# Two relational edge passes of a graph network: another order of ScalarE's work in a step

## The reference

```python
h = relu(layernorm(x))
for w, sl, b in ((w1, sl1, b1), (w2, sl2, b2)):      # two relational layers
    xt  = einsum('nd,rde->rne', h, w)                # 8 matrices, one for each type
    msg = xt[edge_type, src]
    h   = relu(segment_sum(msg, dst) + h @ sl + b)
x = x + h
h = relu(layernorm(x))
# a message layer follows: an MLP over (h[src], h[dst], edge_attr), a layer norm of the
# messages, a segment_sum, an MLP over the nodes and a last layer norm
x = x + message_layer(h, src, dst, edge_attr)
```

## Time and profile before

| | |
|---|---|
| runs, median | 2863.91 us |
| profiled execution | 2855.17 us, span 2853.5 us |
| busy in the span | PE 77%, DVE 71%, POOL 64%, ACT 54% |
| E1, 230 to 795 us | PE 494.08, DVE 425.04, ACT 326.71, POOL 383.09 us busy, granted clock 0.97, DMA share 0.49 |
| E2, 965 to 1520 us | PE 468.39, DVE 367.56, ACT 242.44, POOL 417.32 us busy, granted clock 0.96, DMA share 0.44 |

### The profile page before, as it was taken

The page is one execution under the profiler, slowest core; times in us unless marked ns, Lnnn a source line. Parts: engine busy times, 40 slices in busy tenths (PEclk is TensorE's granted clock), DMA queues, the critical chain, the costliest instruction groups (busy, mean ns, idle before and its releaser), DMA issues. The chain is left out here.

```text
span 2853.5 us, 54165 instructions
## 1 busy us (share of the span) xinstructions
PE 2187.5 (77%) x16219; PEld 1892.5 (66%) x16219; DVE 2023.0 (71%) x6854; ACT 1541.0 (54%) x3284; POOL 1821.7 (64%) x1381
## 2 busy tenths in 40 slices
PE   4778999999668899889873665577767766757997
PEld 4668988888668798888872565444444444435765
DVE  6887887878423587676755888676767676755999
ACT  5996656565423354444434877544334333425887
POOL 5763878765667188888866777288777777770000
PEclk9999999999889999999996888888888888888999
DMA  7994555545379644444437999666666666647998
GB/s 237 316 310 130 113 111 102 107 89 102 48 264 362 248 86 88 88 82 88 88 46 242 417 417 414 253 195 194 175 176 190 181 182 179 191 113 294 406 404 344
DMA packets 297971, 576.18 MB, mean 202 GB/s; under 512 B 65872, under 2 KB 147344, under 8 KB 297872
## 3 DMA queue, kind: packets, MB, share of 16 engines
q1 hardware_dynamic: 188112, 485.01, 46.9%
q0 software_dynamic: 109760, 90.00, 19.5%
HBM read 368.35 MB, written 206.50 MB: 201 GB/s over the span
## 5 line engine op out<-in xcount | busy, mean ns | idle before, releaser
L1056 POOL DMA_INDIRECT s<-E_summed,c_scat x392 | 652.1, 1664 | 262.6 <-ACT E_summed L1235 150.0
L1284 PE MATMUL ps<-c_w,E_masked 128*128 128x128 f32 x6272 | 722.6, 276 | 2.2 <-DVE E_masked L1087 2.0
L1284 PEld LDWEIGHTS ps<-c_w,E_masked 128*128 128x128 f32 x6272 | 714.1, 193 | 3.0 <-DVE E_masked L1087 3.0
L1087 DVE SCALAR_TENSOR_TENSOR E_masked<-E_type_row,E_hT 128x512 f32<-128x512 int32 x784 | 484.1, 688 | 74.4 <-ACT E_hT L1204 62.5
L365 POOL DMA_INDIRECT E_src_rows<-s,c_src x392 | 419.8, 1071 | 167.8 <-issue 118.0
L1418 POOL DMA_INDIRECT s<-E_summed,c_scat x196 | 335.8, 1713 | 126.3 <-issue 53.3
L1407 POOL DMA_INDIRECT E_ends<-h,c_near x196 | 220.1, 1123 | 91.0 <-issue 58.8
L1641 PE MATMUL ps<-E_same,E_normal 128*128 128x512 f32 (+3 forms) x392 | 175.1, 610 | 115.6 <-DVE E_normal L1501 115.6
L365 POOL DMA_INDIRECT E_src_rows<-in_x,c_src x196 | 191.6, 978 | 105.7 <-issue 74.3
L1235 ACT COPY E_summed<-ps 128x512 f32<-128x512 f32 x98 | 57.4, 586 | 347.1 <-DMA s<-E_summed,c_scat 347.0
L1641 PEld LDWEIGHTS ps<-E_same,E_normal 128*128 128x128 f32 x392 | 97.2, 259 | 222.5 <-DVE E_normal L1501 122.2
(11 more groups left out here) (134 smaller groups left out, 4378.8 us busy)
## 6 DMA issues: line engine op xcount, KB each, us to landing
s<-N_out SPq DMA_DIRECT2D x147, 512.0 KB, 5.3
N_xin<-in_x SPq DMA_DIRECT2D x98, 512.0 KB, 10.2
N_sin<-s SPq DMA_DIRECT2D x98, 512.0 KB, 6.8
E_dst_row<-in_dst_line SPq DMA_DIRECT2D x147, 256.0 KB, 4.5
E_type_row<-in_type SPq DMA_DIRECT2D x98, 256.0 KB, 3.5
N_xin<-s SPq DMA_DIRECT2D x49, 512.0 KB, 6.3
h<-N_h SPq DMA_DIRECT2D x49, 512.0 KB, 7.8
E_base<-s SPq DMA_DIRECT2D x49, 512.0 KB, 3.6
```

The costliest lines, as they stand in the source:

```text
L1056: pool.indirect_dma_start(s, bass.IndirectOffsetOnAxis(ap=c["scat"][:, k:k + 1], axis=0), summed[:, g % 2, t * D:(t + 1) * D], None, compu ...
L1087: nc.vector.scalar_tensor_tensor(out=masked[:, u % 2, r, :], in0=type_row[:, u, :], scalar=float(r), in1=hT[:, u % 2, :], op0=ALU.is_equal ...
L1284: ins = nc.tensor.matmul(ps[:, 2 + u % 2, t * D:(t + 1) * D], masked[:, u % 2, r, t * P:(t + 1) * P], w[:, r, :], start=(r == 0 and t == 0 ...
```

## The change

In ScalarE's step the equalities go to the end, and the sums behind them; the sums are then those of group g-1 instead of g-2. Normalisation (or the copy of the fetched rows) and the message copy come directly behind the copy of the transposed rows. After the loop one group's sums are left instead of two. All other engines' streams stay as they are, and so do all waits.

```diff
-                l, m, n = ahead(i, u, -2), ahead(i, u, 1), ahead(i, u, 2)
+                l, m, n = ahead(i, u, -1), ahead(i, u, 1), ahead(i, u, 2)
                 if m:
                     turned_rows(*m)
-                if l:
-                    sums(*l)
-                equalities(i, u)
                 if n and norm:
                     ln.deviations(nc, act, c["eps"], n[1], UNROLL * n[0] + n[1])
                     normalise(*n)
                 elif n:
                     fetched(*n)
                 if norm:
                     messages(i, u)
+                equalities(i, u)
+                if l:
+                    sums(*l)
 
             sweep(act, step)
-            for g in (GROUPS_E - 2, GROUPS_E - 1):
-                sums(g // UNROLL, g % UNROLL)
+            sums(GROUPS_E // UNROLL, 0)
```

## The result

The changed kernel is slower: 2935.57 us in the median of four runs (2923.22 to 2940.42) against 2861.14 for the kernel before beside it, **+74 us**; the ratio is 1.030, 95% interval 1.019 to 1.041. I had forecast 2893 within 2846 to 2916: the right side, by the collision I named, and less than half the size. (Runs of the kernel before lie mostly near 2858 and a few, for a reason that stays open, at 2809 to 2841, at the same granted clock; a ratio takes only each kernel's runs within 1.5% of its quickest, so medians of all runs stand beside it.)

A forecast was written before the change was run, and what follows sets the result against it. GpSimd's scatter chain was taken to bound E1, and GpSimd still more plainly E2. Terms: +1.1 start of E1, +33 held scatter DMAs, -5 E2, sum +29 us: 2884 profiled, 2893 median; range 2846 to 2916.

The forecast's parts named there:

- What bounds E1: Edge pass E1: a chain on GpSimd alone, four scatter DMAs issued, the last one landed, then the next four.
- the sums' wait is no lever: E1: sums lie ready a whole period ahead, so copying them sooner was priced at nothing, except +1.1 us at the start.
- Load at 6.37 us: E1: SP's load goes 6.37 us after a group's first scatter DMA instead of 3.82.
- The hold: E1: loads beside the fourth scatter DMA delay its landing; period 12.05 instead of 11.05 over 33 groups, +33 us.
- My two rows: E1 groups at 310.67 and 322.57: load 1.44 us after or 0.56 before the fourth scatter DMA, next group 6.14 and 6.11 later.
- My upper end, 6.14: E1: longest time assumed from fourth scatter DMA to next group; with 6.26 before it, a period of 12.40.
- E2, -5 us: Edge pass E2: masks end before the gathers, so second gathers take 0.98 instead of 1.46; -5 us, bounds -10 and +5.
- The first ten groups: E1 before group 10: not counted, as ScalarE is not yet held by the landings there.
- the loads did not miss the scatter DMA: Rival 1, E1: the load goes 7.4 us or later after the first scatter DMA, which lands alone; -33, 2831 us; chance 0.17.
- TensorE's granted clock: Rival 2, E1: TensorE idles more, its clock falls to 0.75 of full; +33 more, 2926 us; chance 0.06.
- The third rival: Nothing to see: scatter and loads share, or sums' slack hides all; E1 as now, E2 -5, 2860 us; chance 0.15.
- The rule that I set beside it: Trainium skill: DMA engines serve queues in turn, packet by packet; landing stays near 4.59 us wherever E1's loads fall.

The follow-up runs named there:

- experiment 4: The changed kernel with equalities put back ahead of normalisation and message copy, so only the sums are copied sooner: 2876.74 us, +21.
- (2): The kernel before, old ScalarE order, with SP's loads in E1 also waiting for the same group's message copy: 2905.55 us, +50.
- (1): The changed kernel with SP's load of group g in E1 also waiting until scatter g-7 has landed: 2851.06 us.
- (5): The kernel before with E1's loads held for landed scatter DMAs, going ahead of the next group's first one: 2838.82 us, 18.5 below the kernel before.
- experiment 8: The changed kernel with all 49 groups' gathers issued before E1 instead of 36 of them: 2901.86 us (one run).

## Why the prediction was right in direction and wrong in size

- *What bounds E1, and that the sums' wait is no lever:* right for the groups without gathers. Sums alone left E1 at +0.2 us a group (experiment 4); loads alone, in the old order, made most of the loss (2) and took it back in the new order (1). In the groups with gathers the landing was no bound in the kernel before: GpSimd's instructions and the issue between them filled all but 0.30 of 11.04 us.
- *Load at 6.37 us:* measured 6.42 (6.35 to 6.50, groups 10 to 39).
- *The hold, the step that failed:* the forecast took 6.15 us from the fourth scatter DMA to the next group, and 5.9 before it, for all 33 groups. Measured were 6.90 and 6.46 with gathers, 6.41 and 5.98 without: +58.8 us instead of +33. My two rows, loads 0.56 before and 1.44 after the fourth one, gave 6.1 both, and I took what lies between for equally long. They lie on the two flanks; the table has its top, about 7, at 0, where the change puts the load in the groups with gathers; at +0.5, where it stands without them, 6.55. My upper end, 6.14, was a flank too, so the range could not hold it. And I took one 5.9 for both kinds of group, though before already showed 6.08 and 5.88; with gathers the new order made it 6.46. The picture behind it, a DMA held until the loads have drained, was wrong too: the packets of both queues run in turn. And both rows have two gathers behind the fourth one, which with it fill 4.4 us, so the 4.02 of the tail, which has none, was not what to set them against.
- *E2, -5 us:* the wrong sign, +10. I followed the masks off the gathers, and that saving came as estimated (0.23 us a group in the mean); but the scatter DMAs that the masks meet instead, which stood only in the bound (+5), lost 0.52.
- *The first ten groups* I had counted at nothing; from group 7 on they were already held (+5.3).
- *Rivals:* the loads did not miss the scatter DMA. TensorE's granted clock was lower, 0.93 over E1 against 0.97, and TensorE idles more there; that it set no time is argued, not shown: ScalarE's step took the 7.14 us forecast, and GpSimd's scatters wait for landings. The third rival, nothing to see, was out: the same order takes 3.95 us behind the fourth scatter DMA with the loads moved (1) and 6.40 without. The rule that I set beside it is not refuted by that, nor by the earlier trace rows. The Trainium skill ("DMA: Bandwidth & Descriptors", section Queues, rings and completion order) has each DMA engine take its queues in turn, packet by packet, and the trace agrees as far as it shows: 285 packets of SP's run in the 2.4 us in which the scatter DMA's 144 do; it doesn't tell the engines apart. What didn't follow is that sharing costs nothing.

## What to carry to other kernels

Where a chain waits for the landing of a small indirect DMA, look at what each reordering on another engine does to the moment of the bulk transfers, and move these by a wait of their own to right behind the landing: a wait of one line took back the change's whole loss (1) and gave 18 us in the old order (5). Where the chain's engine is full with its own instructions, as in the groups with gathers, there is nothing left to win by that. When a cost depends on the distance of two events, two points on either side of it do not bound what lies between. And an instruction that leaves one collision (masks on gathers) has to be followed to the next (masks on scatter DMAs).

## What was not expected of the hardware

- The same code ran E1 in two rhythms within one execution, 9.9 and 12.2 us a group (experiment 8). The change from the one to the other began with a scatter DMA on GpSimd that started 4.85 us late, at 591.71, while VectorE's eight masks ran without a gap (587.37 to 592.27). Elsewhere a scatter DMA beside masks took mostly no more than 0.6 us longer. Whether the masks caused the late start, or the late start the change of rhythm, is not shown: both are read from the order of events in one run. The Trainium skill ("SBUF — State Buffer", section Who interferes with whom) has a VectorE instruction with two SBUF inputs contend with a GpSimd instruction that reads SBUF. The 1.83 against 1.55 us in E2 fit that, if an indirect DMA counts as such a read, which no run here shows; the wait of nearly a whole run of masks is longer than one mask of 0.6.
